# GNN attention layer and routed FFN on one core: gather buffers kept from the tables' stage on, three groups gathered there

## The reference

```python
ft = (layernorm(x) @ W).reshape(n, 4, 64)
e = e_src[src] + e_dst[dst]                 # scores of ft for each head
e = jnp.where(e >= 0, e, 0.2 * e)
ex = jnp.exp(e - segment_max(e, dst)[dst])
a = ex / segment_sum(ex, dst)[dst] * dist
x = x + segment_sum(ft[src] * a, dst)
...
x = x + routed_ffn(layernorm(x))            # top 2 of 6 experts, three layers each
```

## Time and profile before

| | |
|---|---|
| median of 3 runs | 3205.76 us (3198.64 to 3207.13) |
| the profiled execution: its time | 3206.61 us |
| its span, first to last instruction | 3204.9 us |
| granted TensorE clock, mean | 0.859 |
| PE / DVE / ACT / POOL busy in the span | 2353.8 / 1804.5 / 1465.7 / 2190.4 us |
| gathers of the main stage (L975) | 1568, from 219.1 to 2321.0 us |
| start of the experts' block | 2378.85 us |

### The profile page before, as it was taken

One profiled execution on the slowest core, in us unless ns is written; L12 is line 12 of the kernel. 1 busy time (PEld: TensorE's weight loads), 2 busy tenths in 40 slices (PEclk: granted clock), 3 DMA queues, 4 the chain that ended last, 5 costly groups with the idle time before them and its releaser, 6 DMA issues. The chain is left out here.

```text
span 3204.9 us, 61858 instructions
## 1 busy us (share of the span) xinstructions
PE 2353.8 (73%) x15568; PEld 1901.2 (59%) x15569; DVE 1804.5 (56%) x3920; ACT 1465.7 (46%) x2676; POOL 2190.4 (68%) x2064
## 2 busy tenths in 40 slices
PE   4944666766767767777777777777748999898995
PEld 3723445555555556565665656656637777777774
DVE  6843444555555666677677777777769332322332
ACT  2512233333344444445555656666635554444442
POOL 0027777777777777777777777776706777777775
PEclk9967777778787887889789888988969999999998
DMA  5625555555555555556655666565532445454443
GB/s 171 197 79 151 151 157 156 162 170 149 175 169 164 176 165 170 171 178 174 183 172 177 184 176 185 169 180 173 159 98 5 76 78 81 77 80 80 78 79 46
DMA packets 231877, 450.52 MB, mean 141 GB/s; under 512 B 55819, under 2 KB 148783, under 8 KB 230770
## 3 DMA queue, kind: packets, MB, share of 16 engines
q0 software_dynamic: 114816, 265.53, 35.5%
q1 hardware_dynamic: 76616, 140.14, 13.5%
q10 hardware_dynamic: 39924, 38.86, 3.7%
HBM read 376.74 MB, written 69.01 MB: 139 GB/s over the span
## 5 line engine op out<-in xcount | busy, mean ns | idle before, releaser
L975 POOL DMA_INDIRECT m_rows<-table,src_col x1568 | 1600.9, 1021 | 541.9 <-issue 506.1
L1361 PE MATMUL m_A<-m_msg,m_by_edge 128*128 128x260 f32 x3920 | 1187.3, 467 | 264.7 <-issue 210.4
L1361 PEld LDWEIGHTS m_A<-m_msg,m_by_edge 128*128 128x128 f32 x3920 | 899.4, 236 | 462.6 <-issue 279.9
L1215 ACT ACTIVATE m_apart<-m_drow,nid 128x1024 bf16 x297 | 341.0, 1148 | 766.3 <-SPq L943 692.5
L1051 DVE TENSOR_TENSOR m_msg<-m_rows,m_A 128x2048 f32<-128x2048 f32 (+1 forms) x294 | 568.1, 1932 | 115.4 <-issue 108.9
L1347 PEld LDWEIGHTS m_E<-m_look_parts,m_by_node 128*128 128x128 bf16 x7104 | 233.0, 97 | 332.8 <-issue 296.4
L1347 PE MATMUL m_E<-m_look_parts,m_by_node 128*128 x7104 | 246.9, 167 | 245.9 <-ACT m_by_node L1218 245.1
L1569 POOL DMA_INDIRECT out<-x_con,x_to_i x206 | 329.2, 1598 | 111.3 <-issue 75.8
L1027 DVE TENSOR_TENSOR m_z<-m_E,m_rows 128x64 f32<-128x64 f32 x295 | 66.0, 224 | 572.0 <-PE m_E L1347 418.9
L1218 ACT ACTIVATE m_by_node<-m_apart,m_one 128x1024 bf16<-128x1024 bf16 x297 | 340.9, 1148 | 9.7
L1011 DVE SCALAR_TENSOR_TENSOR m_by_edge<-dst_col,m_less_base,row 128x1024 f32<-128x1024 f32 (+1 forms) x295 | 325.4, 1103 | 0.6 <-issue 0.4
(11 more groups left out here) (245 smaller groups left out, 2192.7 us busy)
## 6 DMA issues: line engine op xcount, KB each, us to landing
m_drow<-edges SPq DMA_DIRECT2D x196, 512.0 KB
m_rows<-table,src_col POOLq DMA_INDIRECT x1568
table<-f_rowbuf SPq DMA_DIRECT2D x14, 924.0 KB, 5.0
ydram<-m_y ACTq DMA_DIRECT2D x49, 264.0 KB
m_xb<-in_x ACTq DMA_DIRECT2D x48, 256.0 KB
out<-m_x ACTq DMA_DIRECT2D x48, 256.0 KB
f_xin<-in_x SPq DMA_DIRECT2D x13, 896.0 KB, 6.9
x_w<-in_L_ffn_expert_w SPq DMA_DIRECT2D x18, 256.0 KB, 5.5
```

Source lines behind the costliest of these rows:

```text
L975: nc.gpsimd.indirect_dma_start(rows[:, g % RING, j, :], None, table, bass.IndirectOffsetOnAxis(ap=K.src_col[:, g, j:j + 1], axis=0)).then_ ...
L1215: a.activation(apart[i][:, :], drow[:, bass.ds(g % RING, 1), :].rearrange("p a n -> p (a n)"), ACT.Abs, bias=K.nid[:, bass.ds(b, 1)], scal ...
L1361: m = t.matmul(psA[i][:, 0:MSG], by_edge[i][:, j, :], msg[i][:, j, :], start=(j == tiles[0]), stop=(j == tiles[-1]))
```

## The change

`rows`, `drow`, the router's weights `r1`, `r2`, `rb` and their semaphores are no longer made in the main block. They are made once for the whole kernel (`K.rows` and so on), so that they exist in the blocks before. Then:

- SP, at the start of `edge_tables`, issues the four first broadcasts and the three weight loads, and only then waits for the plan that it stores. The same seven DMAs go from the start of the main block.
- POOL, in `edge_tables`, waits for the four copies that fill `src_col` and gathers groups 0 and 1. In `lookup_table` it gathers group 2. In the main block its loop begins with group 3.
- The gather's code becomes a function. Ring, waits, and the order within the main loop are as before.

```diff
 RING = 4
+AHEAD = 3
...
+def gather(nc, K, table, g):
+
+    for j in range(GT):
+        nc.gpsimd.indirect_dma_start(
+            K.rows[:, g % RING, j, :], None, table,
+            bass.IndirectOffsetOnAxis(ap=K.src_col[:, g, j:j + 1], axis=0)).then_inc(K.gathered[g % RING], 16)
...
         @block.sync
         def _(sp):
+            for i in range(RING):
+                sp.dma_start(K.drow[:, i, :], edges[1, i * GE:(i + 1) * GE].partition_broadcast(P)).then_inc(K.spread_row[i], 16)
+            rw1, rb1, rw2, rb2 = w[0:4]
+            sp.dma_start(K.r1[:, :, :], rw1.rearrange("(c p) n -> p c n", p=P)).then_inc(K.weights_in, 16)
+            sp.dma_start(K.r2[:, :], rw2).then_inc(K.weights_in, 16)
+            sp.dma_start(K.rb[:, :], rb1.rearrange("(p a) -> p a", a=1)).then_inc(K.weights_in, 16)
             sp.wait_ge(asked, 6)
             sp.dma_start(sched, tab_i[:, :]).then_inc(stored, 16)
             sp.wait_ge(stored, 16)
...
             nc.gpsimd.iota(brow_i[:, :], [[1, 1]], base=0, channel_multiplier=1).then_inc(consts, 1)
+            pool.wait_ge(copied, 4)
+            for g in range(AHEAD - 1):
+                gather(nc, K, table, g)
...
+        @block.gpsimd
+        def _(pool):
+            gather(nc, K, table, AHEAD - 1)
...
-            for i in range(RING):
-                spread(i * GE, i)
-            sp.dma_start(r1[:, :, :], rw1.rearrange("(c p) n -> p c n", p=P)).then_inc(weights_in, 16)
-            sp.dma_start(r2[:, :], rw2).then_inc(weights_in, 16)
-            sp.dma_start(rb[:, :], rb1.rearrange("(p a) -> p a", a=1)).then_inc(weights_in, 16)
             for i in range(RING - 1):
                 announce(0, i)
...
-            for g in range(NG):
+            for g in range(AHEAD, NG):
                 if g >= RING:
                     pool.wait_ge(gathered[g % RING], 16 * GT * (g // RING))
                     pool.wait_ge(slot_free, g - RING + 1)
-                gather(g)
+                gather(nc, K, table, g)
```

More of the change, by code:

```diff
@@ L415, in _, with edge_tables @@
                 st.settle()
-def edge_tables(nc, edges, K, sched):
+def gather(nc, K, table, g):
[3 more added lines that the diff above has]
+            bass.IndirectOffsetOnAxis(ap=K.src_col[:, g, j:j + 1], axis=0)).then_inc(K.gathered[g % RING], 16)
+def edge_tables(nc, edges, K, sched, table, w):
     with ExitStack() as ctx:
@@ L594, in _, with lookup_table @@
             v.nop().then_inc(asked, 1)
-def lookup_table(nc, K):
+def lookup_table(nc, K, table):
     with ExitStack() as ctx:
@@ L869, in main_stage @@
 def main_stage(nc, K, table, x, sched, ydram, w, out):
-    rw1, rb1, rw2, rb2 = w[0:4]
     with ExitStack() as ctx:
@@ L878, in sem @@
             return ctx.enter_context(nc.semaphore("m_" + n))
-        rows = sb("rows", [P, RING, GT, ROW])
-        drow = sb("drow", [P, RING, GE])
+        rows, drow = K.rows, K.drow
         by_edge = [sb(f"by_edge{i}", [P, GT, P]) for i in range(3)]
@@ L889, in main_stage @@
         sums = sb("sums", [P, AR, MSG])
-        r1, rb = sb("r1", [P, 2, RH]), sb("rb", [P, 1])
-        r2 = sb("r2", [P, NX])
+        r1, r2, rb = K.r1, K.r2, K.rb
         none = sb("none", [P, 2])
@@ L909, in main_stage @@
         wd = [a[:, 320:320 + GT * HEADS].rearrange("p (j h) -> p j h", h=HEADS) for a in psA]
-        gathered = [sem(f"gathered{i}") for i in range(RING)]
-        spread_row = [sem(f"spread_row{i}") for i in range(RING)]
+        gathered, spread_row, weights_in = K.gathered, K.spread_row, K.weights_in
         gathers_seen = sem("gathers_seen")
@@ L921, in main_stage @@
         light_steps, apart_made, node_onehots = sem("light_steps"), sem("apart_made"), sem("node_onehots")
-        weights_in, ready = sem("weights_in"), sem("ready")
+        ready = sem("ready")
         x_in, y_made, y_turned, y_copied = sem("x_in"), sem("y_made"), sem("y_turned"), sem("y_copied")
@@ L1900, in gnn_ffn_kernel @@
         K.lg = sb("lg", [P, NB, NX])
+        K.rows, K.drow = sb("rows", [P, RING, GT, ROW]), sb("drow", [P, RING, GE])
+        K.r1, K.r2, K.rb = sb("r1", [P, 2, RH]), sb("r2", [P, NX]), sb("rb", [P, 1])
+        K.gathered = [ctx.enter_context(nc.semaphore(f"gathered{i}")) for i in range(RING)]
+        K.spread_row = [ctx.enter_context(nc.semaphore(f"spread_row{i}")) for i in range(RING)]
+        K.weights_in = ctx.enter_context(nc.semaphore("weights_in"))
         K.dst_col, K.dist_col = sb("dst_col", [P, NG, GT]), sb("dist_col", [P, NG, GT])
@@ L1910, in gnn_ffn_kernel @@
             sort_edges(nc, K, edges, sorted_edges)
-            edge_tables(nc, edges, K, sched)
-            lookup_table(nc, K)
+            edge_tables(nc, edges, K, sched, table, w)
+            lookup_table(nc, K, table)
         exact_bounds(nc, K, table, sched)
```

## The result

The changed kernel takes 3182.18 us (median of 5 runs, 3177.45 to 3187.67) where the kernel before took 3203.31 beside it (5 runs, 3194.04 to 3207.13): **ratio 0.9940, 95% interval 0.9919 to 0.9961**. On a second chip it was 3181.26 against 3194.85, ratio 0.9951 (0.9936 to 0.9967). So it is faster, by 21.1 and 13.6 us in the medians.

What follows compares the result with a forecast made beforehand. POOL's row of 1568 gathers was taken to pace the main stage. Group 4's 46.0 us into the main block, less 19.0 and the 5.4 later block start, gave 21.6 us off 3206.61: forecast 3185 us, range 3176 to 3197.

Steps and rivals of the forecast that it cites:

- The bound and the rule: Main stage: POOL's row of gathers sets its time; the end moves as much as group 4's first gather.
- engines behind: Rival, main stage: PE and DVE set the end, head start only stored in the ring; 3208 us, 3200 to 3215 0.06.
- The main block begins later: Before the main block: early gathers lengthen tables' stage by 0.3 and look-up stage by 5.1 us; 5.4 together (4.4 to 11.6).
- the drain: End of the look-up block: POOL's drain behind its last gather, given 0 to 2 us and taken as 0.
- Within the main block: POOL idles some 5 us for slot 0; group 4 starts 19.0 us into the block (18.4 to 21).
- The sum: At group 4 and the end: 46.0 - 19.0 - 5.4 = 21.6 us earlier, bounds 13.4 to 23.2.
- DVE held by gathers: Rival, tables' stage: 41 DVE instructions each held up to 0.95 us, 39 in all, 3224 us; chance 0.05.
- The item is not earlier: Rival, main block: item 0 starts as before, group 4 4.2 us later, 3189, or 3197; late item or part-held DVE 0.12.

Runs made afterwards that it cites:

- e5: Changed kernel plus 16 spare gathers into an unread buffer before group 3 in the main block; ratio 1.0005 to the kernel before.
- e6: Changed kernel plus 16 spare gathers, placed before group 100 or before group 180; ratios 1.0024 and 1.0015 to the kernel before.
- e4: Changed kernel plus a POOL wait, ending the look-up block, until group 2's gathers have landed; executed once, group 4 at 66.0 us.
- c0: The changed kernel run again, unedited, on a second chip; 3181.26 us, ratio 0.9951 to the kernel before.
- e1: Changed kernel with both early gather calls taken out, only the seven loads early; ratio 1.0000 to the kernel before.
- e2: Changed kernel with the seven DMAs moved back to the main block, only the gathers early; ratio 0.9971 to the kernel before.
- e8: Changed kernel with 15 gathers in the tables' stage, 3 in the look-up stage, 14 in the main block; ratio 0.9931 to the kernel before.
- e9: Changed kernel with tables' and look-up stages as one block holding 18 gathers; 3182.38 against 3205.95 us before, ratio 0.9932; on a slow chip 0.9922.

## Why the prediction was right, and where it was not

**The bound and the rule** held. POOL's row paces the main stage, and the place of group 4 gives the end (table; e5, e6). The rival "engines behind" predicted no gain and falls on the chips that ran the kernel in some 3200 us: with e5 and e6 nearly all of the extra work in the row came out at its end.

**The main block begins later**: forecast 5.4 us, measured 47.1 - 38.1 = 9.0. The gathers' part was right: first one 8.0 us into the stage as forecast, the 16th through at 207.29 + 1.94 - 179.77 = 29.5, as forecast; in the look-up stage POOL ends 221.95 + 0.95 - 217.65 = 5.3 us behind DVE, forecast 5.1. What was mis-sized is **the drain, set to 0 (bounds 0 to 2, for the look-up stage alone)**. The tables' stage was to end 0.3 us later and ends 32.3 - 30.4 = 1.9 later (the next stage's first DVE instruction, from the iota); the look-up stage was to be 5.1 us longer and is 14.8 - 7.7 = 7.1 longer. In the tables' stage a rival would be that the gathers in flight delay the landing of the plan's store. SP's waits at the end of that stage exclude it. After:

```profile
SPq L431 <- PEq L431: 1.8, 1, 1.8
SPq L431 <- DMA sched<-et_tab_i: 1.2, 1, 1.2
```

Before:

```profile
SPq L422 <- DMA sched<-et_tab_i: 1.2, 1, 1.2
...
SPq L422 <- PEq L422: 0.2, 1, 0.2
```

The store takes as long as before; what is new is that SP then waits 1.8 us for the others instead of 0.2. The last to come is POOL: its last gather ends at 209.23, its DRAIN at 211.77, the next stage begins at 212.06. (PEq is only one of the engines that raise the semaphore of the meeting.) Behind the last gather of the look-up stage (222.90) the plan load comes 3.95 us later, where it came 216.74 - 214.64 = 2.1 behind DVE's last instruction. So the drain is worth some 1.6 us on the path in the first stage and 1.9 in the second, together nearly all of the missing 9.0 - 5.4 = 3.6. It ends with the landing of the gathers (e4). A drain behind instructions that transfer data was taken from rows in which nothing was transferred.

**Within the main block** group 4 was put at 19.0 and came at 245.25 - 226.85 = 18.4. ACT began 5.8 us in, the parts were ready at 10.7, the multiply was done at 17.6 (forecast 18.0). POOL stood 6.6 us there instead of 5, since group 3 was out by 11.8.

**The sum**: 46.0 - 18.4 - 9.0 = 18.6 instead of 21.6, within its bounds (13.4 to 23.2). That 3185 lies only 2.8 us from 3182.18 is partly luck; the second comparison gained 13.6 us, not 21.1. In the pair of profiles the span fell by 23.3: 18.6 at group 4, 3.6 between it and the experts, 2.2 in the experts, less 1.1 that the earlier stages took longer. The last three vary as much between two runs of the same code (after and c0: 2.9, 3.6 and 0.8).

**DVE held by gathers**: as a cause of lost time it falls, but DVE is held a little. The plan's store comes 208.49 - 179.77 = 28.7 us into the stage, 28.5 before: 0.2 us for 41 instructions. Two of the 41 take 0.2 us longer than before, and both began while a gather was under way. From POOL's and DVE's timelines after:

```profile
199.29 0.95 POOL L422 DMA_INDIRECT rows<-table,src_col  x1 [0.30 <-issue]
199.84 0.54 DVE L567 TENSOR_SCALAR et_flat_g<-et_flat_g 1x320 f32<-1x320 f32 x1
...
205.91 1.07 POOL L422 DMA_INDIRECT rows<-table,src_col  x1 [0.30 <-issue]
206.60 1.81 DVE L610 CAST et_tab_i<-et_tab 1x2779 int32<-1x2779 f32 x1
```

The same two before:

```profile
198.67 0.32 DVE L549 TENSOR_SCALAR et_flat_g<-et_flat_g 1x320 f32<-1x320 f32 x1
...
205.46 1.59 DVE L592 CAST et_tab_i<-et_tab 1x2779 int32<-1x2779 f32 x1
```

What the first one lost was taken up by the wait for PE behind it; what the second lost reached the store. The same two are 0.2 us longer in every other run that gathers in this stage, but for the one on the slow chip, where only the cast is; in e1, which does not gather there, they are not. By the Trainium skill (SBUF — State Buffer, "Who interferes with whom") whichever of the two issues first holds the shared pair of ports for its whole instruction and the other is blocked, if DVE is in a 2-port mode; whether these two were, the trace does not show. Had DVE been blocked to the end of the running gather, the two would have lost 0.40 and 0.39 us; they lost 0.22 and 0.21. The other way round the trace agrees: the gather that began inside the cast (207.29) took 1.94, longer by 1.0. So what the prediction read from the earlier trace rows, that DVE is not held, is not true of every instruction; the rival's price of up to 0.95 us for each of 41 was far too high.

**The item is not earlier**: e2 is that rival made real. Its price was 4.2 us and is 7.3: ACT starts 1.3 us later than before, and its exponential behind three pairs of one-hots (with the second look-up 1.3 us of waiting) had been counted only for the case in which ACT starts early.

## What to carry to other kernels

Find the row of instructions that paces a stage, take one landmark in it (here the first gather that both versions issue with the ring in the same state), and predict that landmark. Its move was the gain here, within the scatter, and it can be read to 0.1 us where the time scatters by 10. Work moved ahead of a barrier is free only up to where the other engines end, and the landing of what it issued counts in: here POOL was ready to leave a block 2.0 to 2.6 us after the end of its last gather. Cut the early work to that, or take the barrier away; at group 4 both brought more than the change (e8, e9), in the time neither was shown to. Two halves of a change that each shorten a chain into the same wait must be priced together.

## What the runs showed that was not expected

- POOL's first gather of the whole kernel comes 2.4 us (before) and 2.2 us (e1) into the main block; in every version that had gathered in an earlier block it comes at 0.7. In the tables' stage, where POOL had waited 7.34 us for its indices, the first one started 0.3 us after them. What the 1.5 us are was not tried.
- One chip ran the main stage 700 us longer, with holes between PE's single matmuls and a granted clock of 0.72 between 1000 and 1100 us (0.80 in the first run of e9, same stretch). Its experts' stage took 829 us, on the others 816 to 826.
- POOL's DRAIN at a block's end finished a nearly fixed time after the last gather's data had landed, 0.37 us in the look-up stage and 0.70 in the tables' (e4).
